# A four-layer attention and feed-forward kernel: the first block's steps in another order, and matmuls that nothing reads in TensorE's gaps

## The reference

```python
x = x + _L0_xattn_ref(_layernorm(x), ctx_768, ...)   # first block: top-32 scores -> FiLM ("conditioning"), a 512-tap
                                                     # convolution by FFT, FiLM again, a 4x feed-forward, layer norm
x = x + _L0_ffn_ref(_layernorm(x), ...)              # second: 4 of 16 heads chosen by the mean token, attention
x = x + _L1_xattn_ref(_layernorm(x), ctx_768, ...)   # third: attention with scores normalised by mean and variance
x = x + _L1_ffn_ref(_layernorm(x), ...)              # fourth: a tile picked per token, small splines
x = x + _L2_xattn_ref(ctx_768, _layernorm(x), ...)   # fifth: latent attention
x = x + _L2_ffn_ref(_layernorm(x), ...)              # sixth: 8 experts and 2 shared ones, all computed
x = x + _L3_xattn_ref(_layernorm(x), ctx_768, ...)   # seventh: 16 heads on the context
x = x + _L3_ffn_ref(_layernorm(x), ...)              # eighth: ternary feed-forward
```

```python
c_t = einsum('btg,bgd->btd', attn.mean(heads), x_vision @ Wv)
scale_in, shift_in = split(c_t @ W_film_in + b_film_in);  x = x * (1 + gate * scale_in) + gate * shift_in
Kf = rfft(K, n=2 * L);  xf = rfft(x, n=2 * L);  y = irfft(xf * Kf)[:L] + x * D_skip
scale_out, shift_out = split(c_t @ W_film_out + b_film_out);  y = y * (1 + gate * scale_out) + gate * shift_out
xt = x_text + y;  xt = xt + gelu(layernorm(xt) @ W1 + b1) @ W2 + b2
```

## Time and profile before

| | before |
|---|---|
| median of 3 runs | 609.62 us (607.9 to 612.11) |
| the profiled execution | 607.13 us |
| its span, first to last instruction | 605.3 us |
| mean granted TensorE clock | 0.856 of 2.4 GHz |
| busy: PE, DVE, ACT, POOL | 480.0, 382.4, 270.3, 148.4 us |
| share of the chain that ended last: PE, DVE, ACT, POOL, issue | 58%, 13%, 4%, 4%, 2% |

### The profile page before, as it was taken

How to read it: one execution, slowest core, us unless ns; L and a number is a source line. 1 busy time by engine, 2 the same in 40 slices (tenths; PEclk the granted TensorE clock), 3 DMA queues, 4 the chain that set the end, 5 groups by cost and what they waited for, 6 DMA issues and landing times.

```text
span 605.3 us, 9093 instructions
## 1 busy us (share of the span) xinstructions
PE 480.0 (79%) x3027; PEld 338.1 (56%) x3027; DVE 382.4 (63%) x1361; ACT 270.3 (45%) x839; POOL 148.4 (25%) x179
## 2 busy tenths in 40 slices
PE   3940579799845899965768657979999999789976
PEld 2310579687613476654556434756666666458845
DVE  4999975344675567744758346774444444699866
ACT  2588563511323566613344434632222222398553
POOL 4979970031165000002102440110000000300032
PEclk9665779799966999985655778997999999899999
DMA  7002000001290000000010130000000000000001
GB/s 273 26 21 119 2 3 2 0 1 61 87 392 1 1 2 1 2 2 0 0 32 11 33 94 1 2 1 0 2 1 1 1 0 1 1 1 1 3 1 35
DMA packets 8196, 18.35 MB, mean 30 GB/s; under 512 B 1043, under 2 KB 6227, under 8 KB 7638
## 3 DMA queue, kind: packets, MB, share of 16 engines
q1 hardware_dynamic: 8150, 17.78, 8.3%
HBM read 15.99 MB, written 1.79 MB: 29 GB/s over the span
## 4 chain that ended last, share of the span: by engine, by line
PE 58%; DVE 13%; ACT 4%; POOL 4%; issue 2%; ACTq 0%; DVEq 0%
PE bank L1764 6%; PE bank L1765 6%; PE bank L1775 6%; PE bank L1019 3%; PE bank L759 3%; PE bank L1950 3%; PE bank L1063 3%; PE bank L1042 2%; POOL rstd L205 2%; ACT arenaB L1966 2%; PE bank L728 2%; PE bank L1926 2%; DVE stats L196 2%; PE bank L1638 2%; PE bank L970 2%
## 5 line engine op out<-in xcount | busy, mean ns | idle before, releaser
L204 POOL TENSOR_SCALAR rtmp<-mv 128x4 f32<-128x4 f32 x22 | 5.1, 230 | 327.7 <-DVE mv L190 327.7
L1816 DVE TENSOR_TENSOR arenaB<-arenaB,bank 128x512 f32<-128x512 f32 x40 | 27.5, 688 | 54.7 <-PE bank L1765 53.8
L1786 ACT ACTIVATE arenaB<-bank 128x512 f32<-128x512 f32 x40 | 23.9, 598 | 76.7 <-PE bank L1764 76.7
L1775 PEld LDWEIGHTS bank<-arenaA,arenaB 128*128 128x128 f32 x320 | 38.7, 192 | 9.1 <-issue 9.1
L1764 PE MATMUL bank<-xnT,arenaA 128*128 128x512 f32 x80 | 42.8, 617 | 0.0
L1765 PE MATMUL bank<-xnT,arenaA 128*128 128x512 f32 x80 | 41.7, 604 | 0.0
L1775 PE MATMUL bank<-arenaA,arenaB 128*128 128x128 f32 x320 | 38.8, 275 | 0.0
L478 PE MATMUL bank<-diag,arenaB 128*77 128x128 f32 x64 | 10.8, 339 | 30.7 <-ACT diag L446 27.2
L1966 ACT ACTIVATE arenaB<-bank,arenaB 128x77 f32<-128x77 f32 x88 | 27.1, 348 | 5.1 <-DVE arenaB L1989 5.1
L1074 DVE TENSOR_REDUCE nmax<-bank 128x1 f32<-128x512 f32 x32 | 20.5, 684 | 11.1 <-PE bank L1019 11.1
L478 PEld LDWEIGHTS bank<-diag,arenaB 128*77 128x77 f32 x64 | 10.0, 195 | 31.1 <-issue 31.1
(11 more groups left out here) (468 smaller groups left out, 1264.8 us busy)
## 6 DMA issues: line engine op xcount, KB each, us to landing
arenaA<-in_moe_dram SPq DMA_DIRECT2D x1, 3840.0 KB, 11.5
in_dft<-in_dft_dram SPq DMA_DIRECT2D x1, 2048.0 KB, 7.9
in_dft<-in_head_dram SPq DMA_DIRECT2D x1, 2048.0 KB, 7.5
arenaA<-in_l_dram SPq DMA_DIRECT2D x1, 2048.0 KB, 16.0
vw_scratch<-in_dft SPq DMA_DIRECT2D x32, 38.5 KB
arenaB<-vw_scratch SPq DMA_DIRECT2D x2, 576.0 KB, 4.8
in_rows<-in_rows_dram SPq DMA_DIRECT2D x1, 842.5 KB, 6.9
in_ctx<-in_ctx_dram SPq DMA_DIRECT2D x1, 653.0 KB, 5.2
```

What stands on the lines that cost most here:

```text
L1775: ins = nc.tensor.matmul(bank[4 + m % 3][:, q4 * P:(q4 + 1) * P], hid2[:, m % 2, c, q4 * P:(q4 + 1) * P], w[:, 2 * HE + c * P:2 * HE + (c ...
L1786: nc.scalar.activation(sil2[:, n % 3, :], bank[n % 2][:], ACT.Silu).then_inc(silu_ready, 1)
L1816: Vv.tensor_tensor(hid2[:, m % 2, c, :], sil2[:, n % 3, :], bank[2 + n % 2][:], ALU.mult).then_inc(hid_ready, 1)
```

## The change

There are two edits that can be told apart.

**The first block in another order.** `pe_dft_k`, the kernel's transform, is called behind `pe_kernel(3)` and ahead of `pe_film(1)`; the way back of batch 0 is called ahead of `pe_film(3)`; the feed-forward's way up of batch 0 is called ahead of the way back of batch 1. For this `pe_nyquist`, `act_nyquist` and `vec_nyquist` are split by batch, `act_film` is split in `act_diag` and `act_film`, `pe_ffn0` in `pe_ffn0_up` and the existing `pe_ffn0_down`, and the semaphore counts follow. ScalarE's angles are computed between the score copies, its rows ahead of the first exponentials; POOL's `pool_rstd_twice` moves from the middle of `pool_s4` to ahead of it, and its gains and rows ahead of `pool_x2(0)`. The packed columns (`cols`) share the semaphore of the tokens' load, which five DMAs now raise, and no longer that of the context. VectorE calls `vec_s4_columns` ahead of all of `vec_top(1)`, and `vec_spectrum(0)` ahead of the last rounds of `vec_top(3)`.

**Matmuls that nothing reads.** `pe_spin(into, n, width)` issues n float32 matmuls of the identity with the packed context's first columns, 128 wide or (with `S`) 512 wide, into a bank that holds nothing at that time. No one waits for them and they wait for no one. They stand at 13 places from `pe_c2` to the fifth block's folded weights: 57 matmuls in all, 34 of them 512 wide and 23 of them 128 wide.

```diff
@@ LOADS, packs
-LOADS = [("cols", "ctx"), ("rows",), ("s4",), ("l2", "l3f", "l1"), ("dft",), ("ffn0", "small0"), ("head0",), ("moe", "l3")]
+LOADS = [("ctx",), ("rows",), ("s4",), ("l2", "l3f", "l1"), ("dft",), ("ffn0", "small0"), ("head0",), ("moe", "l3")]
...
+        loaded["cols"] = (x_loaded, 16 * (1 + P // LA))
@@ new
+        def pe_spin(into, n, width=P):
+
+            for _ in range(n):
+                nc.tensor.matmul(bank[into][:, 0:width], ident, packed["ctx"][:, 0:width], start=True, stop=True)
@@ pe_route
                 nc.tensor.matmul(bank[2 + b][0:HF, :], wr, xnT[:, b * S:(b + 1) * S], start=True, stop=True).then_inc(route_pe, 1)
+            pe_spin(6, 3)
             pe.wait_ge(route_vec, 1)
             nc.tensor.transpose(bank[4][0:NB, 0:HF], dist[:], ident[0:HF, 0:HF]).then_inc(route_pe, 1)
+            pe_spin(6, 8, S)
@@ pe_l1x
                 pe_turn(pe, ln_done, NT * 4, xn, [b])
+                pe_spin(6, 2)
                 pe.wait_ge(ln_T, NB * 3 + b + 1)
...
                 ins.then_inc(s1_mm, 1)
+                pe_spin(6, 4)
...
             nc.tensor.matmul(bank[4][:, 0:NB], V["avg"], mv1[:, :, 0], start=True, stop=True).then_inc(avg1_mm, 1)
+            pe_spin(6, 2)
             pe.wait_ge(l1x_vec, 2)
             nc.tensor.matmul(bank[5][:, 0:NB], V["avg"], vr1[:], start=True, stop=True).then_inc(avg1_mm, 1)
+            pe_spin(6, 6)
@@ pe_l1f
             ins.then_inc(l1f_pe, 1)
+            pe_spin(1, 4, S)
             pe.wait_ge(*loaded["l3"])
             pe.wait_ge(l1f_vec, 2)
             pe_fold3(pe, *FOLD3[0])
+            pe_spin(1, 2, S)
             pe_fold3(pe, *FOLD3[1])
+            pe_spin(1, 2, S)
@@ tensor block
             pe_fold1(pe)
-            pe_film(pe, 0)
             pe_kernel(pe, 0)
             pe_kernel(pe, 1)
+            pe_kernel(pe, 2)
+            pe_film(pe, 0)
+            pe_kernel(pe, 3)
+            pe_dft_k(pe)
             pe_film(pe, 1)
-            pe_kernel(pe, 2)
-            pe_dft_x(pe, 0, range(2))
-            pe_kernel(pe, 3)
-            pe_dft_x(pe, 0, range(2, TB))
-            pe_dft_k(pe)
+            pe_dft_x(pe, 0, range(TB))
+            pe_nyquist(pe, 0)
             pe_film(pe, 2)
-            pe.wait_ge(kf_ready, 1)
+            pe_dft_back(pe, 0)
+            pe.wait_ge(kf_ready, 2)
             pe_dft_x(pe, 1, range(2))
             pe_film(pe, 3)
-            pe_nyquist(pe)
+            pe_nyquist(pe, 1)
             pe_dft_x(pe, 1, range(2, TB))
-            pe_dft_back(pe, 0)
+            pe_turn(pe, ln_done, NT * 1, tmp2, [0])
+            pe_ffn0_up(pe, 0)
             pe_dft_back(pe, 1)
-            pe_ffn0(pe)
+            pe_turn(pe, ln_done, NT * 1, tmp2, [1])
+            pe_ffn0_down(pe, 0)
+            pe_ffn0_up(pe, 1)
+            pe_ffn0_down(pe, 1)
             pe_weights3(pe)
             pe_c2(pe)
+            pe_spin(6, 5, S)
             pe_turn(pe, ln_done, NT * 3, xn)
...
             pe_l1x(pe)
+            pe_spin(2, 4, S)
             pe_turn(pe, ln_done, NT * 5, xn)
             pe_l1f(pe)
+            pe_spin(1, 5, S)
             pe_turn(pe, ln_done, NT * 7, tmp2)
@@ scalar block
             act_s4_tanh(act)
-            act_scores0(act, range(TB))
+            act_scores0(act, range(2))
+            act_s4_angles(act)
+            act_scores0(act, range(2, TB))
...
             act_x2(act)
-            act_exps0(act, 0)
-            act_vfilm(act)
-            act_fold1(act)
-            act_s4_angles(act)
             act_s4_columns(act)
             act_s4_turns(act)
             act_s4_rows(act)
+            act_exps0(act, 0)
             act_sums0(act, 0)
+            act_vfilm(act)
+            act_fold1(act)
+            act_kernel(act, 0)
             act_exps0(act, 1)
+            act_kernel(act, 1)
             act_sums0(act, 1)
+            act_diag(act, 0)
             act_film(act, 0)
...
@@ gpsimd block
             pool_masks(pool, st)
+            pool_rstd_twice(pool, st, 0, False)
             pool_s4(pool, st)
+            pool_s4_gains(pool, st)
+            pool_gate(pool)
+            pool_s4_rows(pool, st, range(4))
             pool_x2(pool, st, 0)
-            pool_gate(pool)
-            pool_s4_gains(pool, st)
-            pool_s4_rows(pool, st, range(4))
@@ vector block
-            vec_top(dve, st, 1, range(1))
             vec_s4_columns(dve)
-            vec_top(dve, st, 1, range(1, 4))
+            vec_top(dve, st, 1, range(4))
...
             vec_weight0(dve, st, 2)
+            vec_spectrum(dve, st, 0)
+            vec_nyquist(dve, 0)
             vec_top(dve, st, 3, range(2, 4))
             vec_mask0(dve, 3)
             vec_film(dve, st, 2)
             vec_weight0(dve, st, 3)
-            vec_spectrum(dve, st, 0)
             vec_film(dve, st, 3)
-            vec_nyquist(dve)
-            vec_spectrum(dve, st, 1)
+            vec_nyquist(dve, 1)
             vec_xt(dve, st, 0)
             vec_normalise(dve, 1, xt, tmp2, [0])
+            vec_spectrum(dve, st, 1)
```

84 lines of the change are left out of this document (44 added, 40 removed).

## The result

The change took **602.16 us** (median of 4 runs, 599.54 to 606.65) against 609.49: a ratio of 0.9892, 95% interval 0.9843 to 0.994. That is 1.1% faster where I had forecast 2.3% (595). It lies inside my range of 585 to 604, but the mechanism gave only half of what I had worked out. Ratios here are over fast executions alone and aren't the quotient of the medians beside them. The profiled execution is the slowest of the four (606.65, span 604.8), so I read it beside a second profiled one of the same kernel (604.62) from the experiments.

The account below looks back on a forecast made before the run. TensorE at half clock in chains of small matmuls (165 to 360 us) was taken as the bound. Unread matmuls -13, first block's front -0.6 and end -0.7 made -14.3 us: 609.6 to 595, range 585 to 604.

Parts of the forecast that it names:

- -13: Second to fifth blocks: gain from unread matmuls keeping the clock up, 16.3 us less 3.3, between 0 and 16.
- All fit or nearly fit at 2.4 GHz: Groups of unread matmuls: each is hidden by its wait, at 0.93 us a wide and 0.24 a narrow one.
- Rival 2: Unread groups: the clock does not rise in them and they are late by 24.3 us, 632 us; chance 0.07.
- twice the one-hot turn and lookup, 4.0: Fourth block: one-hot turn (1.06) and lookup (2.94) halve, twice, giving 4.0 of the block's 5.8 us.
- I take off 3.3 us for stretches in which the clock falls between the groups: Between the unread groups: 3.3 us off the 16.3, also for groups late because they start at 1.2 GHz.
- Second block, 4.5, and the third's turn, 0.5: Second block: turn 0.6, routing matmuls 1.7, first projections 2.2 us gained; third block's turn 0.55.
- Third block, 2.6: Third block behind its turn: scores gain 1.0 us and the product 1.6 of its 3.78.
- First block, front part: Up to the last conditioning: kernel's transform starts at S = 78.5, break-even 80.3; -0.6 us, between -4 and +6.
- First block, end: Frequency step to last way down: 43.4 us becomes 39.3, plus 3.4 charged for clock falls in two waits; -0.7 us.
- my own signs: Forecast wrong if wide groups end after their waits or the first block ends elsewhere than at 162 to 166 us.
- rival 1: Between the groups the clock falls anyway; second block gains fully (4.5), the rest half (4.2): 600 to 604; chance 0.14.
- Rival 3: Clock's fall is worth little on the path, 2.63 us on two links, 5.3 us: 604; chance 0.07.

Follow-up runs that it names:

- spins_only: The kernel before with only the 57 unread matmuls added at the same places: 603.88 us, ratio 0.9906.
- all_filled_old_order: The fuller set of unread matmuls on the order of the kernel before, without the two fillings of the first block: 593.84 us, ratio 0.9767.
- trimmed: filled_end with three groups of wide unread matmuls cut (8 to 6, 4 to 3, 4 to 2): 596.25 us, ratio 0.9734.
- order_only: The changed kernel with every unread matmul left out, the first block in its new order: 612.25 us, ratio 1.0031.
- lookup_up: filled_end with four instead of two wide unread matmuls behind the second fold, ahead of the one-hots' turn: 596.81 us, ratio 0.9805.
- later_too: filled_end with 11 more wide unread matmuls in waits of later stages that the change leaves alone: 594.44 us, ratio 0.9723.
- the three with everything: Unread matmuls of the earlier runs put together on three orders of the first block: 591.72, 593.84 and 588.77 us.
- last_wait_filled: all_filled_up_behind with nine instead of five wide unread matmuls ahead of the fifth block's turn: 587.81 us, ratio 0.9668.
- filled_end: The changed kernel with 3 wide unread matmuls ahead of batch 0's turn and 4 ahead of batch 1's, ending the first block: 600.8 us, ratio 0.9832.
- all_filled_up_behind: Everything together on the new order, batch 1's way back again ahead of batch 0's turn and way up, four unread matmuls ahead of it: 588.77 us, 0.9679.

## Why the prediction was right in its direction and wrong in its size

**What bounds the kernel: right.** The small matmuls at half clock between 165 and 360 us were on the path: raising the clock there, and nothing else, gave 0.94% (spins_only), and with more waits filled and the late groups cut 2.3% (all_filled_old_order), 14 of the 16.3 us that I had summed up. Some of that lies behind the experts, where I had counted nothing.

**"-13" for the unread matmuls: the step that failed.** The matmuls gave 5.7 us on the old order, and on the new one 1.36%, some 8 us (0.9895 against 1.0031). The mechanism was right and the term was mis-sized. Two things that it rests on did not hold, and a third may not have.

First, "All fit or nearly fit at 2.4 GHz". I priced every group at 0.93 us a matmul, while three of the eight wide groups ran in part at 1.2 GHz and took 8.83, 5.87 and 5.40 us. Rival 2 had this price, but I took it as all or nothing. (Its 632 is laid on the profiled execution; on the median, as the other rivals are, it is 634.) Ahead of the folded weights cutting the group from four to two gave about 2.4 us back. Ahead of the fourth block's turn it was late by about 1 us and raised the clock for what follows (L1300 1.98 where the earlier trace rows has 3.53, more than the 1.2 that I allowed for it), so there it is even, as trimmed shows.

Second, "twice the one-hot turn and lookup, 4.0". This was the largest single item, and it gave nothing: the group of two ended 2.2 us ahead of the turn, and the clock fell at the end of that rest (1.00 up to 312 us, 0.56 in the next). A group that fills half of a wait may give nothing at all. With four, and two narrow ones in the small waits, the same step took 5.6 us (304.4 to 310.0) instead of 9.3: 3.7 of my 4.0.

Third, "I take off 3.3 us for stretches in which the clock falls between the groups". I looked for these between 165 and 360 us only, and took the stages behind as unchanged. From the experts to the output it took 2.9 and 2.7 us more in the two executions of the change. That the change causes this isn't shown. In the profiled executions of eight kernels that leave this stretch alone it takes 192.0 to 196.9 us; order_only, whose stages ahead are no faster, has 196.8, trimmed and lookup_up, whose stages ahead are, have 192.0, and 192.3 before is one execution at the low end. With its waits filled it takes 191.2 (later_too), 190.1 (the three with everything) and 191.0 (last_wait_filled). The granted clock of the stretch goes with it: 0.94 at 196.8 and 196.9 us, 0.95 at 195, 0.97 at 192, 1.00 at 190.1. So it moves by up to 5 us between executions with where the clock falls, filling its waits makes it shortest, and how much of my missing gain went this way stays open.

**Second block, 4.5, and the third's turn, 0.5: 1.6 and 1.8.** The projections took 3.60 and 3.67, as foreseen, and their 2.2 us are there. The routing's 1.7 are not: from its first matmul to the projections it is 13.1 and 12.6 us, before 12.3. In one execution the routing took 1.89, but the clock fell as the group of 8 began; in the other the group took 7.13, but the clock was down for the routing (3.42). In later_too neither happened, and it is 11.4. Half of the turn (0.6) was no gain anywhere, since its two parts wait for VectorE each.

**Third block, 2.6: 1.9 and 1.3.** The scores' part is there (1.12 where the earlier trace rows has 1.99). The product was to give 1.6 of its 3.78 us and took 3.17 and 3.78: the clock fell ahead of it, at 278 us in the first execution, behind narrow groups and waits of under 0.4 us. In later_too it took 2.05, with all filled 3.78 again; no kernel here keeps the clock up for it reliably, so a half-filled wait isn't the only place where it falls.

**First block, front part: -0.6 against +1.4 and +1.0.** The queue was nearly right (41.8 forecast; 40.7 from 82.34 to the last conditioning's end at 123.04). The start S was not: 82.3 and 81.9 where I had laid 78.5, beyond the break-even of 80.3. But the loss is no larger than the scatter: before, the last conditioning ended at 121.6, and with the same order in spins_only and all_filled_old_order at 123.2 and 123.0. VectorE's timeline of the kernel after has the waits for the conditioning of group 1, at 92 us, for which I had said 8 (6.68), and of the last group (8.29):

```profile
92.04 0.29 DVE L715 SCALAR_TENSOR_TENSOR arenaA<-bank,tmp 128x128 f32<-128x128 f32 x1 [6.68 <-PE bank L486]
...
121.86 0.29 DVE L715 SCALAR_TENSOR_TENSOR arenaA<-bank,tmp 128x128 f32<-128x128 f32 x1 [8.29 <-PE bank L486]
```

**First block, end: 42.7 us forecast, 44.1 and 43.0 measured** (from the start of the frequency step, as the prediction counts; 43.3 before). Without falls of the clock I had 39.3; filled_end has 39.0, so the working of the order was right. The 3.4 us that I charged for the falls were too few: "I charge 1.3 of them", but both were paid, with 2.3 and 2.3 us on the way up and down in one execution, 2.8 and 0.9 in the other, and about 0.6 on each turn. The waits themselves were shorter than my 4.4 and 4.7 (2.66 and 3.74 us), and the clock fell all the same. And I weighed the new order against the old one only, not against the change less its last swap, which takes 36.7 us with the clock kept (121.8 to 158.5). With the swap TensorE waits for both turns (2.66 and 3.74); without it, once, for VectorE's products (4.37), since batch 0's turn and way up stand where the second wait would be.

**What was to show it.** By my own signs the forecast was wrong: three groups of wide matmuls ended after their waits, and the block ended at 167.7 and 166.2 us, outside 162 to 166. The projections took 3.60 us, as said; the mean clock is 0.888 and 0.898 instead of above 0.92, and the lookups took 2.94 instead of 1.5.

**The rivals.** The result lies where rival 1 had it (600 to 604): the clock fell anyway between the groups. What it had wrong is the place: the second block was to gain fully, 4.5, and with the third's turn it gave 1.6 and 1.8. Nor are groups of four and more wide ones too short for the clock to rise: in the change it rose within each one that ran into the lower level. Rival 3, that the clock is worth little, falls: with the groups placed well they give 2.3% by themselves. The Trainium skill (TensorE: Matmul & The Clock Gate, Part 1: The HAM clock gate, What's actually happening) says that for modelling, the ramp penalty is under 1% of a typical kernel's span. The first result, 0.94% for the matmuls alone, seems to agree, but the trace and the fillings don't bear it out as a bound here: the lower level comes back again and again (174 us of it before), and removing more of it gave 2.3%. I gave rival 1 only 0.14, and the forecast 0.50, as though the groups' sizes were a detail. They were the result.

## What to carry to other kernels

Unread matmuls in TensorE's waits are a real tool for a kernel whose small steps run in a chain at half clock, worth 2.3% here; but each group is to be sized by the wait it stands in as the trace shows it *after* the groups ahead are in, with room for a clock that may fall as it begins (8 took 7.13 or 8.83 us), and one that fills half of a wait can be worth nothing while one that is late costs directly. Look at the stages that you didn't touch too: falls of the clock there moved the end by up to 5 us between executions, which can hide or feign a gain. When steps are moved, ask which real work is left to stand in each new wait, and whether a PSUM bank is free there for matmuls that nothing reads.

## What the runs showed that I had not expected

The same program differs between executions by up to 9 us (598.2 to 607.2 us in six of the change, granted clock 0.890 to 0.915), and the kernel before by up to 8 (606.8 to 614.5 in 23). Where the profiled ones differ, it is by single falls of the clock: the same lookups take 1.57 or 2.94 us, the same scores at L1937 1.56 or 2.85. With the waits filled the single times lie within 5 to 7 us (585.2 to 591.2 in all_filled_up_behind). A stage ahead of the experts, read from one execution, is good to about 2 us, unless a named row in it changes; the long one behind them only to 5. The start of the first block has such a spread of its own: the kernel transform began anywhere from 80.5 to 83.4 us in eleven profiled executions whose kernels are alike up to there.
